# Half steps spread among the whole ones, and one shared step moved from the expert phase to the begin of attention

## The chip, the cores and the metric

The kernel runs on one core of a Trainium2 chip. The metric is the time of one execution on the device, in microseconds, the median of several runs.

## What is computed

A transformer block on 16 batches of 512 rows of 256 numbers, float32:

```python
xn = layernorm(x)
# attention: Q, K, V = relu(xn @ W + b), 16 heads, causal, masked softmax
att = gamma * normalise(softmax(Q K^T / 4) V + xn) + beta
# experts: 8 routed ones, each row goes to its best 2, and one shared by all rows
shared = (silu(xn @ sw1) * (xn @ sw3)) @ sw2
moe = sum over the row's 2 experts of cw * (silu(xn @ w1[e]) * (xn @ w3[e])) @ w2[e]
out = x + att + moe + shared
```

Every matrix of the experts is 256x512 or 512x256. To keep float32's precision each operand of a product is cut into a high and a low part of a narrower format, and a product is made as three matmuls: high by high, high by low, low by high.

## The kernel before

There are two phases, each a block of five programs, one for each engine, that meet in counting semaphores. The order of work within an engine is written out by hand.

**Attention (`attention_phase`).** The body runs for i = -3 to 16. In iteration i it attends batch i, computes the row maxima of batch i+1, projects batch i+2 and normalises batch i+3, each where such a batch exists. An iteration has 44 slots s, and tables (`AT_K`, `AT_V`, ...) say at which slot an engine does which piece. So at i = -3 and i = -2 there is only setup, norm and projection, and at i = -1 the row maxima of batch 0 come in. SP's queue issues all loads and stores in order; `load_aug` loads the augmented queries and keys of a batch with 14 DMAs for each half. Rows of the norm are scattered by GpSimd to `expert_rows`, sorted by expert.

**Experts (`ffn_phase`).** Its work is a series of steps. Step 0 is the shared expert on batch 0. Steps 1 to 39 are the routed chunks: 32 whole ones (512 rows of one expert) and then 7 half ones (256 rows). Steps 40 to 54 are the shared expert on batches 1 to 15. Each step n has four tiles m of 128 hidden columns. TensorE does, in this order: up product of tile 0 (`up(n, 0)`), transposes of the next step's rows, the down products of the step before (`down(n-1)`), up products of tiles 1 to 3. For each tile ScalarE computes silu (`sil`), VectorE multiplies (`hf`), ScalarE copies the high part (`hid_h`) and VectorE subtracts to get the low part (`hid_l`). `down` waits for the last `hid_l` of its step; the up product of a tile waits for `h_done` of the tile two before, whose bank it takes.

Around that, in each routed step:

- ScalarE (`cut_high`) and GpSimd (`cut_low`) cut the next step's weights into high and low, in six pieces of 128x512. TensorE's next step begins when four are cut.
- SP loads the rows of step n+2, stores the result of step n-1 (after ScalarE's `copy_result`), and loads the weights of step n+2.
- Attention's second layer norm is spread over pairs of steps, one batch for each pair. SP's `load_norm` brings its rows in an odd step and `load_residual` the residual; GpSimd's `norm_sum`, `norm_root` and `norm_beta`, VectorE's `norm_centre` and ScalarE's `norm_squares` run in the even step behind; ScalarE's `norm_scale`, GpSimd's `norm_end` and SP's `store_norm` in the step after that. The loads of a norm take the tiles of the one before:

```python
def load_norm(pair):
    sp.wait_ge(norm_read, pair)
...
def norm_end(pair):
    pool.wait_ge(y_scaled, pair)
    pool.wait_ge(res_ready, pair)
    pool.wait_ge(norm_stored, 16 * pair)
    gp.tensor_tensor(out_whole, out_y, out_res, ALU.add).then_inc(norm_read, 1)
```

In the shared steps GpSimd gathers each row's two expert results by indirect DMA, and VectorE adds them, weighted, to the output tile (`complete`), and adds the shared result (`add_shared`).

Of the kernel before, what the change touches and what calls it, by code (L numbers as in the profile page):

```python
# [92 lines left out]
def attention_phase(nc, t, part_dram, xn_dram, expert_rows, plan):  # L93
# [28 lines left out]
    with ExitStack() as ctx:  # L122
# [6 lines left out]
        def sem(name):  # L129
# [34 lines left out]
        q_aug = [sb(f"q_aug{i}", [P, H, S], BF16) for i in range(2)]  # L164
# [6 lines left out]
        negT = sb("negT", [P, 2, 2, Q], BF16)  # L171
        pT = [sb(f"pT{j}", [P, GH, S - P * j]) for j in range(NT)]
        oTs = sb("oTs", [P, 2, S])
        rsum = sb("rsum", [P, NT, GH])

        brow, browp, rw_sb = oTs[0:1, 0], oTs[0:1, 1], pT[0][0:E, 0, 0:C]
        y = sb("y", [P, NT, C])

        logits = sb("logits", [P, B, NT, E])
        xrow = sb("xrow", [P, 2, NT, C])  # L180
# [12 lines left out]

        s_ps = [ps(f"s_ps{i}", [P, S]) for i in range(3)]
        st_ps = [ps(f"st_ps{i}", [P, S]) for i in range(2)]
        misc = [ps(f"misc{i}", [P, 512]) for i in range(2)]
        oT = ps("oT", [P, 512])

# [13 lines left out]
             "filled gate_differs gate_grown").split()]  # L212

# [67 lines left out]

        def group_at(i):
            return (i - 2) // GB if i >= 2 and (i - 2) % GB == 0 and i < B else None
# [30 lines left out]
        def _(sp):  # L314
# [55 lines left out]
            def load_early_rows():  # L370

                sp.dma_start(plan["raw"][:, 3 * 4 * C:].rearrange("p (t c) -> p t c", c=C),
                             xn_dram[0].rearrange("(t p) c -> p t c", p=P)).then_inc(plan["x_in"], 16)
# [31 lines left out]
            def body(i, par, tail, attend, maxima, project, norm):  # L405
                if maxima:
# [234 lines left out]
        def _(act):  # L641
# [36 lines left out]
            def key_ones(k):  # L678

                await_(act, ones_ready, 1)  # L680
                rows_ = k_aug[k][ROW_MASK:P].rearrange("p h (a n) -> p (h a) n", n=P)
                fn(rows_, ones[ROW_MASK:P].rearrange("p (o n) -> p o n", o=1).to_broadcast([P - ROW_MASK, H * S // P, P]),
                   ACT.Copy).then_inc(pads, 1)

            key_ones(0)
# [9 lines left out]
            def body(i, par, tail, attend, maxima, project, norm):  # L695
                for s in range(NU):
# [19 lines left out]
                    if s == AT_SQUARE and norm:  # L716
                        await_(act, a_ready, i + 4)
                        fn(ln_t[:], ln_a[:], ACT.Square).then_inc(sq_done, 1)
                        if i == -3:
                            key_ones(1)  # L720
# [11 lines left out]
        def _(dve):  # L732
# [58 lines left out]
            def weights(s):  # L791
# [7 lines left out]
                if s == AT_ROUTER:  # L799
                    split_router()  # L800

# [343 lines left out]
            def body(i, par, tail, attend, maxima, project, norm):  # L1145
                for s in range(NU):
# [6 lines left out]
                    if tail:  # L1153
                        if s == AT_NORMALISE[3]:
                            normalise(i - 1, 3)
                    if project:
# [73 lines left out]
                    if i == -3:  # L1230
                        weights(s)

# [3 lines left out]
        def _(pe):  # L1236
# [35 lines left out]

            def row_scores(b, par, u):

                if u % NU2 == 0:
# [32 lines left out]
            def weigh(b, par, g, pair):  # L1308

                if (g, pair) == (0, 0):  # L1310
                    await_(pe, vaug_done, b + 1)
                await_(pe, exp_done, NU * b + last_unit[g, 2 * pair + 1] + 1)
# [26 lines left out]
            def body(i, par, tail, attend, maxima, project, norm):  # L1339
                for s in range(NU):  # L1340
# [8 lines left out]
                    if project:  # L1349
# [20 lines left out]
                        if s == AT_K[3]:  # L1370
                            await_(pe, qf_ready, 2 * NC * b + 1)
                            project_tile(b, 3)
                    if s == AT_ROWS[0] and attend:
# [53 lines left out]
def ffn_phase(nc, t, part_dram, xn_dram, expert_rows, plan, out):  # L1427
# [17 lines left out]
    STEPS = CHUNKS + B  # L1445
    assert CHUNKS % 2 == 1 and WHOLE == 2 * B and HALVES >= 2
    ACC, GOT = 4, 3
    first_sum = nc.dram_tensor("first_sum", (S, C), F32, kind="Internal").ap()
    expert_results = nc.dram_tensor("expert_results", (WHOLE * S + HALVES * S // 2, C), F32, kind="Internal").ap()

    with ExitStack() as ctx:
# [51 lines left out]

        def width(n):

            return S // 2 if known(n) and WHOLE < n <= CHUNKS else S
# [5 lines left out]
        def routed(engine, step, written_out=False):  # L1512
# [6 lines left out]
            for n in range(1, 5):  # L1519
                step(n, n % 2, (n + 1) // 2, 1 if n >= 3 else None)  # L1520
            if written_out:
                for n in range(5, 2 * B + 1):
                    step(n, n % 2, (n + 1) // 2, (n - 1) // 2)
            else:
                with engine.Fori(2, B) as pair:
                    for odd in range(2):
                        step(pair * 2 + odd + 1, 1 - odd, pair + 1, pair)
# [582 lines left out]
```

## Time and profile before

| | |
|---|---|
| time, median of 3 runs | 1851.2 us (1849.96 to 1851.47) |
| the profiled execution's own time | 1853.11 us |
| its span | 1851.3 us |
| TensorE busy | 1708.6 us, 92% |
| VectorE, ScalarE, GpSimd busy | 1267.1, 1091.7, 1178.7 us |
| TensorE's granted clock over the span | 0.976 of full |

The span is the time from the first to the last instruction that the profile saw. PE is TensorE, PEld its weight load, DVE VectorE, ACT ScalarE, POOL GpSimd, SP the queue that issues DMAs. A busy share is an average over two phases with different limits, so single stretches matter more. Times in a timeline are microseconds from the span's begin. `early_*` and `w_*` are the two buffers of weights, of the even and the odd steps.

### The profile page before, as it was taken

The page shows a single profiled execution, that of the slowest core. Times are in us where ns is not written, and L with a number is a line of the kernel's source. Part 1 is how long each engine was busy: PE and PEld are TensorE (multiplying, and loading weights), DVE is VectorE, ACT ScalarE, POOL GpSimd, SP SyncE. Part 2 cuts the span into 40 slices and gives each one's busy share as a digit, 9 for nine tenths or more (in the row PEclk, how much of TensorE's full clock was granted, in tenths as well). Part 3 has the DMA queues.
Part 4 walks back from the last instruction along what each step waited for, and adds up shares of the span by engine and source line. Part 5 has one row for each costly group of instructions (what it writes and reads, how often), then busy time and mean ns, then how long its engine had stood idle before and what let it go on. Part 6 is the DMA issues. An engine that isn't in the chain of part 4 may idle for free.

```text
span 1851.3 us, 35725 instructions
## 1 busy us (share of the span) xinstructions
PE 1708.6 (92%) x12066; PEld 1287.0 (70%) x12066; DVE 1267.1 (68%) x3089; ACT 1091.7 (59%) x2072; POOL 1178.7 (64%) x1441
## 2 busy tenths in 40 slices
PE   3489999998999899999799999999999999999998
PEld 2255555555555555554488888888888888888887
DVE  6888888888888888877544554455455454566666
ACT  5247567666676566766556666666666666333332
POOL 4466557776677667846257777777777787553443
PEclk9689999999999999999899999999999999999999
DMA  1444445444445454454655766756667675465543
GB/s 54 154 127 122 129 128 173 154 156 157 144 150 162 141 171 150 159 171 172 221 189 180 237 191 201 232 192 212 216 197 222 200 229 188 149 188 149 158 146 99
DMA packets 246374, 313.29 MB, mean 169 GB/s; under 512 B 31546, under 2 KB 210884, under 8 KB 240068
## 3 DMA queue, kind: packets, MB, share of 16 engines
q1 hardware_dynamic: 233924, 277.60, 47.3%
q0 software_dynamic: 12288, 33.57, 5.7%
q8 instruction: 96, 1.57, 0.3%
q14 instruction: 66, 0.54, 0.1%
HBM read 211.70 MB, written 98.86 MB: 168 GB/s over the span
## 4 chain that ended last, share of the span: by engine, by line
PE 47%; ACT 1%; DMA 1%; DVE 1%; POOL 1%; issue 0%; SPq 0%; DVEq 0%; ACTq 0%
PE gu L2006 29%; PE yp L2020 15%; PE xt L1995 2%; DMA early_raw<-in_L_ffn_w_dram 0%; DVE hf L1876 0%; DMA early_raw<-in_L_ffn_sw_dram 0%; ACT early_high L1771 0%; ACT sil L1777 0%; ACT hid_h L1779 0%; POOL early_low L1679 0%; POOL early_down L1679 0%; POOL w_up_l L1679 0%; POOL rows L1740 0%; DVE hid_l L1879 0%; ACT xc L1785 0%
## 5 line engine op out<-in xcount | busy, mean ns | idle before, releaser
L650 ACT ACTIVATE pT<-st_ps 128x512 f32<-128x512 f32 x682 | 368.6, 563 | 265.7 <-PE st_ps L1305 258.9
L923 DVE CUSTOM_DVE_ANT_0 s_ps<-s_ps,masks 128x384 f32<-128x384 f32 (+1 forms) x512 | 314.6, 633 | 39.6 <-PE s_ps L1284 34.1
L2006 PE MATMUL gu<-xc,early_high 128*128 128x512 f32 (+1 forms) x1120 | 337.9, 385 | 2.5 <-DVE xc L1887 1.5
L1876 DVE TENSOR_TENSOR hf<-sil,gu 128x512 f32<-128x512 f32 (+1 forms) x220 | 143.7, 653 | 275.9 <-ACT sil L1777 275.9
L1284 PE MATMUL s_ps<-k_aug,q_aug 97*128 97x512 bf16 (+3 forms) x1024 | 262.2, 309 | 37.9 <-DVE mx L923 23.4
L1303 PE MATMUL st_ps<-q_aug,k_aug 99*128 99x512 bf16 (+1 forms) x992 | 268.9, 303 | 11.8 <-ACT pT L650 6.7
L1879 DVE TENSOR_TENSOR hid_l<-hf,hid_h 128x512 fp32r<-128x512 f32 (+1 forms) x220 | 175.1, 796 | 147.7 <-ACT hid_h L1779 147.7
L2006 PEld LDWEIGHTS gu<-xc,early_high 128*128 128x128 f32 x1120 | 205.4, 190 | 44.4 <-POOL early_low L1679 4.0
L1779 ACT ACTIVATE hid_h<-hf 128x512 fp32r<-128x512 f32 (+1 forms) x220 | 133.1, 605 | 174.2 <-DVE hf L1876 174.2
L1777 ACT ACTIVATE sil<-gu 128x512 f32<-128x512 f32 (+1 forms) x220 | 123.9, 563 | 180.5 <-PE gu L2006 180.5
L2006 PE MATMUL gu<-xc,early_low 128*128 128x512 f32 (+1 forms) x560 | 214.3, 383 | 0.0
L1687 POOL DMA_INDIRECT got<-expert_results,place x128 | 124.1, 969 | 140.6 <-DVE hf L1876 115.4
L2020 PE MATMUL yp<-early_down,hid_h 128*128 128x256 f32 x1072 | 198.6, 287 | 4.7 <-DVE hid_l L1879 3.0
L1305 PE MATMUL st_ps<-masks,identb 128*128 128x128 bf16 x992 | 194.2, 221 | 0.0
L2006 PE MATMUL gu<-xc,w_up_h 128*128 128x512 f32 (+1 forms) x640 | 184.1, 373 | 6.7 <-DVE hf L1876 3.9
L1318 PE MATMUL oT<-pT,v_aug 128*32 128x512 f32 (+3 forms) x2048 | 170.9, 452 | 2.1 <-ACT pT L650 1.3
L2020 PEld LDWEIGHTS yp<-early_down,hid_h 128*128 128x128 f32 x1072 | 167.9, 193 | 6.2 <-DVE hid_l L1879 3.9
L1284 PEld LDWEIGHTS s_ps<-k_aug,q_aug 97*128 97x128 bf16 x1024 | 95.7, 99 | 107.9 <-DVE mx L923 43.9
L482 POOL DMA_INDIRECT expert_rows<-xrow,slot x128 | 126.7, 990 | 63.6 <-issue 30.3
L1679 POOL TENSOR_TENSOR early_low<-early_raw,early_high 128x512 fp32r<-128x512 f32 x80 | 102.3, 1300 | 87.9 <-ACT early_high L1771 87.9
L2020 PE MATMUL yp<-early_down,hid_l 128*128 128x256 f32 x536 | 152.4, 284 | 0.0
L926 DVE TENSOR_REDUCE mx<-s_ps 128x2 f32<-128x512 f32 (+1 forms) x192 | 123.6, 681 | 19.5 <-PE s_ps L1284 18.9
(260 smaller groups left out, 3889.5 us busy)
## 6 DMA issues: line engine op xcount, KB each, us to landing
w_raw<-in_L_ffn_w_dram SPq DMA_DIRECT2D x60, 512.0 KB, 6.5
early_raw<-in_L_ffn_w_dram SPq DMA_DIRECT2D x57, 512.0 KB, 5.7
part_scr<-parts SPq DMA_DIRECT2D x64, 384.0 KB, 3.8
q_aug<-part_scr SPq DMA_DIRECT2D x192, 128.0 KB
k_aug<-part_scr SPq DMA_DIRECT2D x192, 128.0 KB
early_raw<-expert_rows SPq DMA_DIRECT2D x34, 512.0 KB
expert_results<-yo SPq DMA_DIRECT2D x32, 512.0 KB, 3.3
x_sb<-in_L_attn_x_dram SPq DMA_DIRECT2D x16, 512.0 KB, 4.1
```

The source lines that it names most:

```text
L482: gp.indirect_dma_start(expert_rows, bass.IndirectOffsetOnAxis(ap=at, axis=0), xrow[:, b % 2, n], None).then_inc(scattered[b % 2], 16)
L650: fn(pT[j][:, h:h + heads], unit_view(column_bank(b, u), heads, w), ACT.Exp).then_inc(exp_done, 1)
L923: vec.tensor_tensor_reduce(bank[:, 0:keys], bank[:, 0:keys], masks[:, 2 * C + P - keys:2 * C + P], 1.0, LOWEST, ALU.add, ALU.max, mx[:, h ...
L1284: last = mm(v[:, n], q_aug[par][0:ROWS_S, h0 + n, P * q:P * (q + 1)], k_aug[par][0:ROWS_S, h0 + n, 0:keys], start=heads == 1, stop=n == he ...
L1303: mm(v[:, n], k_aug[par][0:ROWS_ST, h, P * j:P * (j + 1)], q_aug[par][0:ROWS_ST, h, P * j:S], start=True, stop=False)
L1305: last = mm(v[:, n, 0:P], identb[:], cmask[:, 1], start=False, stop=True)
L1318: last = mm(oT[32 * n:32 * (n + 1), P * j:S], v_rows[par][:, at:at + 32], pT[j][:, n], start=j == 0, stop=j == NT - 1, tile_position=(0, 3 ...
L1779: fn(hid[par][0][:, m, 0:w], hf[:, m % 2, 0:w], ACT.Copy).then_inc(hh_done, 1)
L1876: vec.tensor_tensor(hf[:, m % 2, 0:w], sil[:, m % 2, 0:w], gu[m % 2][:, 1, 0:w], ALU.mult).then_inc(h_done, 1)
L1879: vec.tensor_tensor(hid[par][1][:, m, 0:w], hf[:, m % 2, 0:w], hid[par][0][:, m, 0:w].bitcast(F32), ALU.subtract).then_inc(hl_done, 1)
L2006: last = mm(gu[m % 2][:, a, 0:width(n)], w_up[wpar][x][:, a, c, P * m:P * (m + 1)], xc[par][:, y, c, 0:width(n)], start=k == 0, stop=k == ...
L2020: last = mm(yp[:, i], hid[par][x][:, m, P * i:P * (i + 1)], w_dn[wpar][y][:, m], start=j == 0, stop=j == 3 * NH - 1)
```

## The change

Two things are done in one kernel.

1. In the expert phase each half step stands behind four whole ones, at steps 5, 10, 15, 20, 25, 30 and 35, in place of 33 to 39. `chunk_of` says which chunk a step takes, and the loop over pairs is written out. Norms begin in even steps that are whole (`NORM_AT`); even half steps (10, 20, 30) have none. In a half step that is odd `norm_end` is put behind all six pieces of `cut_low`.
2. The shared expert on batch 0 is computed in iterations -2 and -1 of attention: weights and x are loaded by SP at the begin into memory that is lent from tiles used later, cut by ScalarE and VectorE, and the four up tiles, silu, products and down products are put at slots of their own. Step 0 of the expert phase takes batch 1 instead, and the last shared steps take batches 2 to 15: there are 54 steps. The completing of batches is redistributed (`COMPLETED`, `LATE`, `TWICE`).

```diff
+        AT_SW_UP, AT_SW_DOWN, AT_SW_ADD = (18, 19, 30, 35), (10, 14), (12, 16)
+        AT_SW_LOW = (34, 11)
+        AT_SW_SILU, AT_SW_HH = (21, 21, 30, 36), (22, 23, 32, 38)
+        AT_SW_H, AT_SW_HL = (20, 21, 27, 31), (22, 24, 28, 33)
+        AT_ONES = 25
...
+            for a, (n, rows_) in enumerate((("sw1", C), ("sw3", C), ("sw2", 2 * C))):
+                sp.dma_start(sw_raw[:, a].rearrange("p (c n) -> p c n", c=rows_ // P),
+                             t[n][0].rearrange("(c p) n -> p c n", p=P)).then_inc(sw_in, 16)
+            sp.dma_start(sw_sum[:], t["x"][0].rearrange("(t p) c -> p t c", p=P)).then_inc(sw_x_in, 16)
...
+                if b == 1 and tt == 0:
+                    await_(sp, sw_added, 2)
...
+            def shared_high():
+                await_(act, sw_in, 48)
+                await_(act, rw_ps, 1)
+                for q in range(SW_PIECES):
+                    high, _, raw = sw_piece(q)
+                    fn(high, raw, ACT.Copy).then_inc(sw_high, 1)
+            def shared_silu(m):
+                await_(act, sw_gu_ready, m + 1)
+                fn(sw_sil[:, m % 2], sw_gu[m % 2][0][:], ACT.Silu).then_inc(sw_silu, 1)
...
+            def shared_h(m):
+                await_(dve, sw_silu, m + 1)
+                vec.tensor_tensor(sw_hf[:, m % 2], sw_sil[:, m % 2], sw_gu[m % 2][1][:], ALU.mult).then_inc(sw_h, 1)
+            def shared_hid_low(m):
+                await_(dve, sw_hh, m + 1)
+                vec.tensor_tensor(sw_hid[1][:, m], sw_hf[:, m % 2], sw_hid[0][:, m].bitcast(F32), ALU.subtract
+                                  ).then_inc(sw_hl, 1)
+            def shared_add(h):
+                await_(dve, sw_y_ready, h + 1)
+                at = sw_sum[:, 2 * h:2 * h + 2]
+                vec.tensor_tensor(at, sw_y, at, ALU.add).then_inc(sw_added, 1)
...
             def row_scores(b, par, u):
+                if b == 0 and u == 2:
+                    await_(pe, sw_h, NH)
...
-    STEPS = CHUNKS + B
+    STEPS = CHUNKS + B - 1
+    COMPLETED, LATE = {3: (0, 1), 4: (2,), 5: (3,)}, 5
+    TWICE = 20
...
+        SPACING = WHOLE // HALVES + 1
+        NO_NORM = tuple(n for n in range(SPACING, CHUNKS + 1, SPACING) if n % 2 == 0)
+        NORM_AT = {n: k + 1 for k, n in enumerate(n for n in range(2, CHUNKS, 2) if n not in NO_NORM)}
+        def half_step(n):
+            return 0 < n <= CHUNKS and n % SPACING == 0
+        def chunk_of(n):
+            return WHOLE + n // SPACING if half_step(n) else n - n // SPACING
...
+            for n in range(1, CHUNKS + 1):
+                step(n, n % 2, NORM_AT.get(n + n % 2), NORM_AT.get(n - 2 + n % 2))
...
                 cut_low(n + 1, 1 - par, (0, 1))
-                if par == 1 and ends is not None:
+                if par == 1 and ends is not None and not half_step(n):
                     norm_end(ends)
                 if par == 0 and begins is not None:
                     norm_root(begins)
                 cut_low(n + 1, 1 - par, range(2, PIECES))
+                if par == 1 and ends is not None and half_step(n):
+                    norm_end(ends)
                 if par == 0 and begins is not None:
                     norm_beta(begins)
...
-                if 2 <= c < 4:
+                for b in COMPLETED.get(c, ()):
                     for k in range(2):
-                        complete(c - 2, k)
+                        complete(b, k)
```

## Rows read from the trace of the kernel before

**Rows 1.** Engines' summary and costliest groups of the page (busy us, mean ns | idle before).
```profile
PE 1708.6 (92%) x12066; PEld 1287.0 (70%) x12066; DVE 1267.1 (68%) x3089; ACT 1091.7 (59%) x2072; POOL 1178.7 (64%) x1441
...
L1876 DVE TENSOR_TENSOR hf<-sil,gu 128x512 f32<-128x512 f32 (+1 forms) x220 | 143.7, 653 | 275.9 <-ACT sil L1777 275.9
```

**Rows 2.** The chain that ended last, expert phase (start us, us, what).
```profile
1455.12 10.97 PE gu L2006 x48
...
1466.96 5.76 PE yp L2020 x48
1472.72 10.99 PE gu L2006 x48
...
1581.41 2.87 PE yp L2020 x24
1584.29 10.91 PE gu L2006 x48
...
1601.83 10.92 PE gu L2006 x48
```

**Rows 3.** Busy times by stretch: step 32 to the end of step 40.
```profile
1480.74:1592.45 111.71, 103.82 (x742) 96.36 (x742) 55.85 (x96) 70.99 (x162) 75.70 (x62) 0.98 0.60 195
```

**Rows 4.** Groups of instructions: the weighted adds of gathered results.
```profile
L1942 DVE SCALAR_TENSOR_TENSOR acc<-got,gate,acc 128x256 f32<-128x256 f32 x128 | 53.4, 479 | 2.1 <-DMA got<-expert_results,place 1.5
```

**Rows 5.** Timeline of PE, first half step, 33 (start us, us, what [idle before]).
```profile
1498.25 0.44 PE L2006 MATMUL gu<-xc,w_up_h 128*128 128x256 f32 x2
...
1501.71 0.48 PE L2020 MATMUL yp<-early_down,hid_h 128*128 128x256 f32 x2 [1.40 <-POOL w_dn_l L1679]
```

**Rows 6.** Timeline of ACT, half step 33.
```profile
1510.45 1.01 ACT L1851 ACTIVATE yo<-yp 128x1024 f32<-128x1024 f32 x1
1511.36 0.37 ACT L1777 ACTIVATE sil<-gu 128x256 f32<-128x256 f32 x1
```

**Rows 7.** Timeline of DVE, half step 33.
```profile
1504.09 1.32 DVE L1879 TENSOR_TENSOR hid_l<-hf,hid_h 128x256 fp32r<-128x256 f32 x1 [0.48 <-ACT hid_h L1779]
...
1511.83 0.42 DVE L1876 TENSOR_TENSOR hf<-sil,gu 128x256 f32<-128x256 f32 x1 [0.57 <-ACT sil L1777]
```

**Rows 8.** Timeline of POOL, half step 33.
```profile
1503.82 2.74 POOL L1679 TENSOR_TENSOR early_low<-early_raw,early_high 128x512 fp32r<-128x512 f32 x2
1507.31 2.41 POOL L1740 TENSOR_TENSOR rows<-rows 128x1024 f32<-128x1024 f32 x1 [0.75 <-ACT rows L1858]
```

**Rows 9.** Timeline of POOL, an odd whole step and the even one behind it.
```profile
1225.62 2.40 POOL L1740 TENSOR_TENSOR rows<-rows 128x1024 f32<-128x1024 f32 x1
...
1236.98 2.85 POOL L1706 TENSOR_TENSOR rows<-rows 128x1024 f32<-128x1024 f32 x1
...
1249.14 2.55 POOL L1679 TENSOR_TENSOR w_up_l<-w_raw,w_up_h 128x512 fp32r<-128x512 f32 x2 [1.04 <-ACT w_up_h L1771]
```

**Rows 10.** Timeline of SP in the odd step of rows 9: issue of the norm's second load.
```profile
1228.66 0.87 SPq L1582 DMA_DIRECT2D rows<-layernorm_rows  x1
```

**Rows 11.** DMA issues from 1226 to 1246 us (KB each, us to landing).
```profile
rows<-attention_sum SPq DMA_DIRECT2D x1, 512.0 KB, 4.4
rows<-layernorm_rows SPq DMA_DIRECT2D x1, 512.0 KB, 5.8
```

**Rows 12.** Timeline of DVE, the even step of rows 9.
```profile
1241.50 1.20 DVE L1901 TENSOR_REDUCE sm<-rows 128x4 f32<-128x1024 f32 x1
```

**Rows 13.** Timeline of ACT, the even step of rows 9.
```profile
1244.96 1.00 ACT L1851 ACTIVATE yo<-yp 128x1024 f32<-128x1024 f32 x1
1246.56 0.60 ACT L1777 ACTIVATE sil<-gu 128x512 f32<-128x512 f32 x1 [0.59 <-PE gu L2006]
```

**Rows 14.** The chain that ended last, step 1 of the expert phase.
```profile
932.72 4.50 PE gu L2006 x12
```

**Rows 15.** Timeline of DVE, iteration -2 of attention.
```profile
51.43 0.18 DVE L834 RECIPROCAL sm<-sm 128x4 f32<-128x4 f32 x1 [2.07 <-POOL sm L526]
...
62.06 1.67 DVE L880 SCALAR_TENSOR_TENSOR xn<-ln_t,sm,ln_q 128x256 f32<-128x256 f32 x4
```

More of the change, by code:

```diff
@@ L163, in attention_phase @@
         vtmp = sb("vtmp", [P, NT, C])
-        q_aug = [sb(f"q_aug{i}", [P, H, S], BF16) for i in range(2)]
+        q_aug0 = sb("q_aug0", [P, H, S], BF16)
         k_aug = [sb(f"k_aug{i}", [P, H, S], BF16) for i in range(2)]
@@ L719, in body @@
                         if i == -3:
-                            key_ones(1)
+                            shared_high()
+                            key_ones(1, 0, H * 3 // 4)
+                    if i == -2:
+                        for m in range(NH):
+                            if s == AT_SW_SILU[m]:
+                                shared_silu(m)
+                        for m in range(NH):
+                            if s == AT_SW_HH[m]:
+                                shared_hid(m)
+                        if s == AT_ONES:
+                            key_ones(1, H * 3 // 4, H // 4).then_inc(pads, 1)
                     if s == AT_COPY[2] and attend:
@@ L1155, in body @@
                             normalise(i - 1, 3)
+                    if i == -2 and s == AT_SW_LOW[1]:
+                        shared_low(range(3, SW_PIECES))
+                    if i == -1 and s in AT_SW_ADD:
+                        shared_add(AT_SW_ADD.index(s))
                     if project:
@@ L1231, in body @@
                         weights(s)
+                        if s == AT_SW_LOW[0]:
+                            shared_low(range(0, 3))
+                    if i == -2:
+                        for m in range(NH):
+                            if s == AT_SW_HL[m]:
+                                shared_hid_low(m)
+                            if s == AT_SW_H[m]:
+                                shared_h(m)
             iterations(dve, body)
@@ L1639, in shared_step @@
             def shared_step(n, par, c):
-                if c == 1:
+                if c == 2:
                     store_result(CHUNKS)
-                    for k in range(3):
+                    store_norm(B)
+                    for k in range(ACC):
                         load_acc(k)
@@ L1659, in _ @@
             load_routed(2, 0)
-            routed(sp, routed_step)
+            routed(routed_step)
             shared(shared_step)
@@ L1691, in gathers @@
             def gathers():
-                for j in range(2 * NT):
-                    pool.wait_ge(h_done, NH * (CHUNKS + 1) + NH - 1 + j // 2)
-                    gather(j // NT, j % NT)
-                for c in range(2, B):
-                    for i in range(NT):
-                        pool.wait_ge(h_done, NH * (CHUNKS + c) + 1 + i)
-                        gather(c, i)
+                for p in range(B * NT):
+                    after = p // 2 if p < TWICE else p - TWICE // 2
+                    pool.wait_ge(h_done, NH * (CHUNKS + 1) + NH - 1 + after)
+                    gather(p // NT, p % NT)
             def norm_sum(pair):
@@ L1756, in _ @@
             pool.wait_ge(params_in, 32)
-            routed(pool, step)
+            routed(step)
             pool.wait_ge(y_stored, 16 * (CHUNKS + 1))
@@ L1862, in _ @@
             first_step()
-            routed(act, routed_step)
+            routed(routed_step)
             shared(shared_step)
@@ L2054, in _ @@
             routed_step(0, 0, None, None)
-            routed(pe, routed_step, written_out=True)
+            routed(routed_step)
             shared(shared_step)
```

162 lines of the change are left out of this document (111 added, 51 removed).

## The prediction, as it was made before the result

> **What bounds the kernel now.** I read the summary of the engines first, then the chain that ended last, then the stretch of the half steps engine by engine. TensorE is busy for 92% of the span [rows 1]. In the expert phase it is more than busy: the chain runs through TensorE alone, one whole step every 17.60 us (10.97 in the up products, 5.76 in the down products of the step before, the rest transposes), and one shared step every 17.54 us [rows 2]. So a step taken out of this phase is worth its full price, and a stall put into it costs its full price. The stretch from the start of step 32 (the last whole one) to the start of step 41 (the second shared one) lasts 111.71 us with TensorE busy for 103.82 [rows 3]; it holds one whole step, seven half steps and one shared step. All that spreading the half steps can win lies there. In the attention phase VectorE and TensorE share the bound, so I count a delay of its begin at its full size.
>
> **The change, part by part.**
>
> *One shared step fewer.* STEPS falls from 55 to 54; the last shared step and all around it stay as they are, so this takes 17.54 us out [rows 2]. The additions of gathered results (`complete`) are moved: two batches one behind the other after step 41. A batch costs VectorE eight instructions of 0.479 us, 3.8 us [rows 4]; two are 7.7 us, against 17.54 us of the step with some 7 us of other VectorE work between them and the next tile that TensorE waits for. I take 0; without that cover it would be 3.8 us once.
>
> *A half step among whole ones.* The trace has one such place, step 33 behind step 32. TensorE starts its first up product at 1498.25 and then stands idle for 1.40 us before the down products of the whole step 32 [rows 5] (the row names a piece of GpSimd, but `hl_done` is waited for at the same place): the up product of a half tile is too short to cover silu, product, high and low of the last tile. At the other end, ScalarE copies the whole result at 1510.45 before silu of tile 2 at 1511.36 [rows 6], and VectorE's product of that tile ends at 1511.83 + 0.42 = 1512.25 [rows 7]; the next step's first up product needs it. From 1498.25 to 1512.3 are 14.05 us. Each of the seven half steps now stands behind a whole one, so each has this length. The order of GpSimd's work in it is changed (norm_end last), but VectorE's product binds at 14.05 anyway.
>
> *The whole step behind it* has the down products of a half step: 17.60 - 5.76 + 2.87 = 14.7 us [rows 2]. Behind the half steps 10, 20 and 30 no layer norm begins or ends, and I take 14.7.
>
> *The whole step behind half steps 5, 15, 25 and 35* is another matter. NORM_AT puts the begin of a norm into steps 6, 16, 26 and 36, and its rows are loaded in the half step before. Two things stand ahead of that load. (1) load_norm waits for norm_read, which the norm_end of the norm before raises; that one now runs in the same half step, behind all six cut_low. In time from the half step's start: GpSimd starts the first two pieces at 1503.82, +5.6, and two pieces take 2.74 [rows 8]; six are done at +13.8; norm_end takes 2.41 [rows 8] and ends at +16.2, when the half step has been over for 2 us. (2) The second load is issued 0.63 us behind the end of norm_end (1225.62 + 2.40 against 1228.66) [rows 9, 10] and the two landed 4.4 and 5.8 us after their issue [rows 11]. That is +21.2 to +22.7, I take +21.9, or 7.9 us into the whole step. GpSimd's norm_sum, 2.85 us [rows 9], is first in its queue, ahead of the cuts of the next weights, and ends at 10.7. From there the chain of the step is as in the trace: VectorE's reduction starts at 1241.50 [rows 12], ScalarE's copy_result at 1244.96, behind the squares (3.46 later) [rows 13]; a half result costs some 0.5 us to copy; silu of tile 1 starts at 1246.56 [rows 13] and GpSimd's fourth piece ends at 1249.14 + 2.55, 5.13 us later [rows 9]. Together 9.1 us, so the weights of the next step are cut at 7.9 + 2.85 + 9.15 = 19.9 us. TensorE would be through with the step at 14.7. It waits for `h_done` of tile 1, then for these weights. Queued behind the waiting norm_sum are all cut_low of the step; behind VectorE's wait for the sum its tiles 1 to 3; behind ScalarE's wait for the row sums copy_result and tile 1, for which TensorE waits.
>
> During such a wait TensorE idles for about 4 us. In step 1, behind a wait of a few us, twelve up products took 4.50 us [rows 14] where a quarter of a whole step's up products is 2.74: the clock had fallen to its lower level. A small part of that lies on this chain, since the cuts come later than the products; I add 0.4 us. So this step has 20.3 us. The Trainium skill (TensorE: Matmul & The Clock Gate, What's actually happening) says that the default clock is the throttled one and activity releases it; here the trace agrees with 4.50 against 2.74. By that rule alone each of the four waits would cost the full 1.8 us, 5 or 6 us more in the sum.
>
> Bounds of this step: from below 16.4 us, if the rows are there in time (in the trace VectorE comes to the reduction at 1241.50, which is 7.2 us into its step, fourteen steps of 17.60 ahead of 1480.74; 9.15 follow); from above 22.4 (5.8 us to land and the full 1.8 of the clock). I take 20.3, from the middle of the landings.
>
> *Sum of the routed part.* Before, step 32 to 40 and six whole steps that will follow half ones: 111.71 + 6 x 17.60 = 217.3. After, the same fifteen steps: 7 x 14.05 + 3 x 14.7 + 4 x 20.3 + 17.54 = 241.2. That is +23.9 us. Even at 14.7 for all seven followers it would be +1.6: the 5 us of idle around step 40 are won back, and seven short covers are paid.
>
> *The first batch's shared step in attention.* TensorE (96 products), ScalarE and GpSimd have room there; VectorE is what counts. It gets six low cuts, four products, four hid_l and two adds, 16 instructions of 128x512, at 0.653 [rows 1] 10.4 us. Much is hidden in waits: VectorE idles 2.07 us before 51.43 [rows 15] alone. Not hidden are, as I read the slots: tile 3's product and hid_l, which stand behind the last norm work at 62.06 [rows 15] and ahead of the first row maximum, with ScalarE's piece between, 2 us; the two adds, 1.3 us; and some 0.7 because values_out(2) now waits for TensorE's tile 2, with the reciprocals behind it. I take +4. Bounds: 1.3 (only the adds) and 10.4 (all). The four loads (2 MB) are issued behind those that the begin waits for, and the wait of load_aug for sw_added ends before SP gets there; I take 0.
>
> The Trainium skill (SBUF, State Buffer; Who interferes with whom) says that a VectorE instruction with two SBUF inputs contends with a GpSimd one that reads SBUF. In the trace hid_l took 1.32 us beside GpSimd's cuts where the product, one input from PSUM, took 0.42 at the same shape [rows 7]. By that rule the four hid_l added in attention could cost up to 3.6 us more, 1865 in all.
>
> **Total.** 23.9 - 17.5 + 4 = +10.4. The profiled execution spans 1851.3 us, as the median of the runs, 1851.2 (its own time is 1853.1, with 1.8 us around the span). So about 1861.7 us.
>
> **Rivals.**
> A. The norm is not late: loads land before GpSimd is ready, and steps 6, 16, 26, 36 have 16.4 us. The sum is then 23.9 - 15.6 - 17.5 + 4 = -5.2, 1846 us. For it: in the trace norm_sum never waits for its rows. Against it: there norm_end runs in the middle of a 17.6 us step. It decides from 16.8 us of that step on down (faster by 0.2%); break-even is at 17.7.
> B. The price is half as large, 16.8 to 18.6 us for that step: 1847.5 to 1855. Landings as short as 4.4 are not enough for it; GpSimd would have to be through 2 us earlier.
> C. The begin of attention bears all of VectorE's new work: 10.4 in place of 4, 1868 us; with the upper bound of the four steps 1876. For it: VectorE is hardly idle there. Against: the waits on GpSimd's small operations are there to be filled.
> D. Spreading wins as meant, with followers at 14.7 and nothing late: 1.6 - 17.5 + 4, 1839 us. The chain that I found speaks against it.
>
> **How the numbers follow.** My case, 1856 to 1867 us, has 0.60; A 0.13, B 0.12, C 0.10, D 0.05. A measurement of this kernel can tell 0.2%, 3.7 us, from no change. Slower: 0.60 + 0.10 + a little of B, 0.72. Within: 0.11. Faster: A and D, 0.17. The range for 8 in 10 leaves out D and half of A below, and the far end of C above: 1846 to 1870. The likeliest case alone has 1856 to 1867.
>
> **What would show it.** Steps 5, 10, ... would start to end in about 14 us with some 1.4 us idle before the down products. Steps 6, 16, 26, 36 would show norm_sum at 7 to 9 us into the step, a wait of GpSimd on the loads ahead of it, and TensorE idle for 4 to 5 us; steps 11, 21, 31 none of it. Steps 39 to 41 would run without the stall of before. The first row maximum would come 2 or 3 us later, and the expert phase would begin 4 us later. The prediction is wrong if norm_sum starts on time, or if the half steps are shorter than 13.6 us, or if attention's begin moves by 8.

## The result

The changed kernel took 1876.2 us (median of 4 runs, 1874.81 to 1878.44), the kernel before 1850.9 beside it (4 runs, 1849.96 to 1851.47). The ratio is 1.0139, with a 95% interval of 1.0125 to 1.0153: slower, as predicted, but by 25 us in place of 10, and outside the range of 1846 to 1870.

The profiled execution of the changed kernel had its own time of 1874.81 us and a span of 1873.1, 21.8 more than the span of before. The sums below are of spans; the 3.5 us between 21.8 and 25.3 are, but for 0.1, how the two profiled executions lie to their medians (the one of before 2.2 above, this one 1.4 below). Two single executions, 9337 us in experiment 1 and 5810 us in experiment 2, lie far outside all others and count in no ratio below.

The page's summary and its group of VectorE's products, which answer to [rows 1]: nothing in the busy times tells of 22 us. TensorE is busy 8.8 us longer, VectorE 0.9 us shorter.

```profile
PE 1717.4 (92%) x12058; PEld 1290.7 (69%) x12058; DVE 1266.2 (68%) x3094; ACT 1095.8 (59%) x2079; POOL 1180.2 (63%) x1441
...
L2028 DVE TENSOR_TENSOR hf<-sil,gu 128x512 f32<-128x512 f32 (+1 forms) x216 | 140.9, 652 | 282.1 <-ACT sil L1929 282.1
```

The transposes of the next step's rows come once in each step, so the distance between them times the steps. Here are those of the changed kernel in steps 14 to 17, of which 15 is a half one: 16.29, 15.56 and 19.38 us.

```profile
1169.14 0.60 PE L2147 MATMUL xt<-ident,early_raw 128*128 128x128 f32 x4
1185.43 1.04 PE L2147 MATMUL xt<-ident,early_raw 128*128 128x128 f32 x8
1200.99 1.04 PE L2147 MATMUL xt<-ident,early_raw 128*128 128x128 f32 x8
1220.37 1.03 PE L2147 MATMUL xt<-ident,early_raw 128*128 128x128 f32 x8
```

Busy times by stretch (columns: stretch, length, then busy us of PE, PEld, DVE, ACT, POOL, granted clock, DMA share, GB/s): those three intervals, and the same three around the even half step 20.

```profile
1169.14:1220.37 51.23, 46.79 (x285) 41.12 (x284) 27.84 (x41) 32.63 (x73) 39.14 (x40) 0.97 0.66 211
1255.74:1302.40 46.66, 45.14 (x285) 40.21 (x284) 18.84 (x31) 28.23 (x55) 28.07 (x21) 1.00 0.63 209
```

By my terms the first is 17.6 + 14.05 + 20.3 = 51.95, the second 17.6 + 14.05 + 14.7 = 46.35. The chain that ended last, in step 16 of the changed kernel, is the one of the prediction up to silu of tile 1; it answers to [rows 8] and to [rows 9, 10, 12, 13].

```profile
1197.37 2.55 POOL rows L1890
1199.92 0.02 issue
1199.94 0.37 SPq L1727
1200.31 0.04 issue
1200.35 5.01 DMA rows<-layernorm_rows
1205.37 0.07 issue
1205.43 2.40 POOL rows L1856
...
1207.93 1.23 DVE sm L2053
...
1213.30 7.24 PE gu L2158 x24
```

norm_end (L1890) ends at 1199.92, the second load is issued at once and lands 5 us later, norm_sum (L1856) starts at 1205.43, and TensorE goes on at 1213.30, after 2.92 us idle. The prediction let the step end with a second wait, for the cuts of the next weights. The fourth of these ends at 1217.45, TensorE takes up the next step at 1217.51 without an idle time, so the two ends fall together. From there back to the step's first up product at 1198.17 are 19.3 us. So this part came nearly as written. What I had not foreseen stands at both ends of the expert phase. First its begin: the first transposes of before and of the changed kernel.

```profile
912.40 1.94 PE L1995 MATMUL xt<-ident,early_raw 128*128 128x128 f32 x8 [4.38 <-PEq L122]
```

```profile
923.23 1.94 PE L2147 MATMUL xt<-ident,early_raw 128*128 128x128 f32 x8 [4.51 <-PEq L122]
```

It comes 10.8 us later, where I had 4. Then the change from the routed steps to the shared ones: the chain that ended last, from step 40 on.

```profile
1617.81 1.03 ACT yo L2003
1618.85 0.02 issue
1618.87 0.36 SPq L1751
1619.22 0.04 issue
1619.27 4.35 DMA attention_sum<-rows
1623.62 0.07 SPq L1720
1623.68 0.04 issue
1623.72 9.40 DMA early_raw<-layernorm_rows
1633.12 0.04 issue
1633.17 1.97 PE xt L2147 x8
```

SP stores the result of step 39, stores the last norm (which in the kernel before was done many steps earlier), issues four loads of acc (L1720, 512 KB each) and only then the load of step 42's rows. It needs 9.4 us to land. TensorE's transposes come 22.18 us behind those before them, the next ones 18.88 and 17.80 us, in place of 17.54: 6.2 us.

The account by spans:

| part | on record | measured |
|---|---|---|
| begin of the expert phase | +4 | +10.8 |
| steps 0 to 2 | 0 | -0.6 |
| seven half steps, their followers, step 40 | +23.9 | +22.4 |
| other whole steps | 0 | +0.8 |
| rows of step 42 late | 0 | +6.2 |
| one shared step fewer | -17.5 | -17.5 |
| tail | 0 | -0.4 |
| sum | +10.4 | +21.7 |

The third line: the seven groups of three intervals last 4 x 31.84 + 78.03 in all with an odd half step and 3 x 46.66 with an even one, 345.4 us; less seven whole steps of 17.6 and with a shared step of 17.54 that is 239.7, where I had 241.2, against 217.3 of before.

### The profile page after: what moved, and what is told of

It reads as the page before. It is cut to its first block, busy times and chain, and to the rows that moved or that the text cites. A ratio compares the mean times of both kernels' runs of the same rounds, so it can differ in the third digit from the quotient of the medians.

```text
span 1873.1 us, 34800 instructions
## 1 busy us (share of the span) xinstructions
PE 1717.4 (92%) x12058; PEld 1290.7 (69%) x12058; DVE 1266.2 (68%) x3094; ACT 1095.8 (59%) x2079; POOL 1180.2 (63%) x1441
## 4 chain that ended last, share of the span: by engine, by line
PE 38%; POOL 5%; ACT 3%; DMA 2%; issue 2%; DVE 1%; SPq 0%; DVEq 0%; POOLq 0%
PE gu L2158 23%; PE yp L2172 13%; PE xt L2147 2%; POOL early_low L1832 1%; DMA rows<-layernorm_rows 1%; POOL early_down L1832 1%; DVE hf L2028 1%; POOL got L1840 1%; ACT sil L1929 1%; POOL rows L1861 1%; ACT hid_h L1931 1%; POOL rows L1890 1%; POOL w_dn_l L1832 1%; POOL rows L1856 1%; DMA early_raw<-layernorm_rows 1%
## 5 line engine op out<-in xcount | busy, mean ns | idle before, releaser
L2158 PE MATMUL gu<-xc,early_high 128*128 128x512 f32 (+1 forms) x1088 | 332.9, 389 | 14.7 <-DVE hf L2028 13.2
L2031 DVE TENSOR_TENSOR hid_l<-hf,hid_h 128x512 fp32r<-128x512 f32 (+1 forms) x216 | 168.8, 782 | 144.8 <-ACT hid_h L1931 144.8
L2158 PEld LDWEIGHTS gu<-xc,early_high 128*128 128x128 f32 x1088 | 200.9, 192 | 58.6 <-DVE hf L2028 13.8
L2158 PE MATMUL gu<-xc,early_low 128*128 128x512 f32 (+1 forms) x544 | 209.9, 386 | 0.0
L2172 PE MATMUL yp<-early_down,hid_h 128*128 128x256 f32 x1040 | 191.7, 286 | 7.5 <-POOL w_dn_l L1832 4.1
L2172 PEld LDWEIGHTS yp<-early_down,hid_h 128*128 128x128 f32 x1040 | 162.2, 192 | 9.8 <-POOL w_dn_l L1832 4.9
L2172 PE MATMUL yp<-early_down,hid_l 128*128 128x256 f32 x520 | 147.2, 283 | 0.0
```

The costliest lines, as they stand in the source:

```text
L2031: vec.tensor_tensor(hid[par][1][:, m, 0:w], hf[:, m % 2, 0:w], hid[par][0][:, m, 0:w].bitcast(F32), ALU.subtract).then_inc(hl_done, 1)
L2158: last = mm(gu[m % 2][:, a, 0:width(n)], w_up[wpar][x][:, a, c, P * m:P * (m + 1)], xc[par][:, y, c, 0:width(n)], start=k == 0, stop=k == ...
L2172: last = mm(yp[:, i], hid[par][x][:, m, P * i:P * (i + 1)], w_dn[wpar][y][:, m], start=j == 0, stop=j == 3 * NH - 1)
```

## The experiments

Each kernel ran with five rounds beside the kernel before. Ratios are to that, with the 95% interval; the changed kernel has 1.0139.

**1. Attention's part alone.** The half steps go back behind the whole ones, and with them the norms' steps, the place of `norm_end` and the last norm's store (the diff shows the line that decides).

```diff
-            return 0 < n <= CHUNKS and n % SPACING == 0
+            return WHOLE < n <= CHUNKS
```

> The shared step of batch 0 stays in attention (54 steps), the half steps go back to 33 to 39. Read from the two traces, the begin of attention costs 12.2 us where it happens (2.4 in the first loads, 4.2 in iteration -2, 5.5 in iteration -1) and the expert phase begins 10.8 us later; one shared step less is -17.5. My account: 1851 + 10.8 - 17.5 = 1844, ratio 0.996, and within 1842 to 1847. If the term on record (4 us) were right and the rest came from the combination with the spread: 1837. If the steps written out one by one cost 0.05 to 0.08 us each (17.68 in place of 17.60 in the trace), the whole steps show 17.68 here too; if spreading costs it, 17.60.

1850.2 us, ratio 0.9995 (0.9986 to 1.0004). The expert phase began at 920.39. My 1844 was missed: one shared step less, -17.5, is eaten up by +8 at the begin, +2 in whole steps of 17.68 us (not from the spread, then), some +2 around step 40 (0.59 of it TensorE's wait for the rows of step 42, ahead of which four loads of acc stand here too) and +3 in the first half step. That last one is a collision. VectorE's hid_l in the first fence below takes 2.61 us, its likes 0.69, and GpSimd's norm_beta in the second runs from 1511.31 to 1513.66:

```profile
1511.60 2.61 DVE L2026 TENSOR_TENSOR hid_l<-hf,hid_h 128x512 fp32r<-128x512 f32 x1 [0.70 <-ACT hid_h L1926]
```

```profile
1511.31 2.35 POOL L1858 TENSOR_TENSOR rows<-rows,beta_b 128x1024 f32<-128x1024 f32 x1
```

hid_l ends 0.55 us behind norm_beta, as if it had not begun before. The Trainium skill (SBUF, State Buffer; Who interferes with whom) calls the port pair that the two share an exclusive lock, and this trace agrees with 2.61 against 0.69. TensorE stood idle there for 3.72 us, in place of 1.40 in the kernel before.

**2. The spread alone**, put into the kernel before: attention as before and 55 steps.

```diff
-            return S // 2 if known(n) and WHOLE < n <= CHUNKS else S
+            return S // 2 if half_step(n) else S
```

> The half steps are spread, the shared step of batch 0 stays in the expert phase (55 steps), attention is that of before. My account from the traces: spreading 22, whole steps 0.05 us longer each 1, late rows of the second shared step up to 6 (here three loads stand behind the store of the last norm, not four): 1851 + 22 + 1 + 4 to 6 = 1878 to 1880, ratio 1.015. By the terms on record, spread alone: 1875. If the stall of the second shared step needs the fourth load: 1874.

1878.3 us, ratio 1.0149 (1.0130 to 1.0167), as expected. So the two parts are nearly separate: 27.5 and -0.6 us, together 26.9 against 25.3 measured. The rows of step 42 were late here as well (an interval of 19.76 us), with three loads of acc.

**3. Rows of step 42 first.**

```diff
                 if c == 2:
+                    load_x(n + 2, xn_dram[c + 2])
                     store_result(CHUNKS)
                     store_norm(B)
...
-                if c < B - 2:
+                if 2 < c < B - 2:
```

> As the changed kernel, but in step 40 the rows of step 42 are loaded ahead of the store of the last norm and of the four loads of acc. My account: the step that shows 22.2 us falls to 17.6 and the one behind it from 18.9 to 17.6, -6 us against the changed kernel: 1870, ratio 1.0105. Rival: the rows are late because the DMA engines are full of gathers and stores then, whatever the order: 1876, ratio 1.014.

1873.1 us, ratio 1.0109 (1.0092 to 1.0127), 5.6 us less by the ratios, 3.1 by the medians. The trace shows the stall gone: 17.68 and 17.54 us.

```profile
1597.60 1.04 PE L2148 MATMUL xt<-ident,early_raw 128*128 128x128 f32 x8
1615.28 1.03 PE L2148 MATMUL xt<-ident,early_raw 128*128 128x128 f32 x8
1632.82 1.04 PE L2148 MATMUL xt<-ident,early_raw 128*128 128x128 f32 x8
```

The order in SP's queue was the cause. The span fell by 1.8 us only, though, because the followers of the half steps 25 and 35 took 20.68 and 20.62 us here and the steps behind them 18.53 and 18.64, 4.0 us more in all than in the changed kernel. TensorE's wait in step 26 was as long as there (2.88 and 2.97 us); what differs is the clock granted behind it, as the same stretch of the changed kernel and of this one shows:

```profile
1354.00:1391.00 37.00, 32.63 (x201) 28.52 (x201) 20.15 (x28) 22.31 (x50) 29.58 (x26) 0.95 0.65 210
```

```profile
1354.00:1391.00 37.00, 32.72 (x193) 28.70 (x193) 19.77 (x27) 22.10 (x50) 29.70 (x26) 0.91 0.65 213
```

**4. norm_end early** in the odd half steps, behind the first two pieces of cut_low.

```diff
-                if par == 1 and ends is not None and not half_step(n):
+                if par == 1 and ends is not None:
                     norm_end(ends)
```

> As the changed kernel, but in the odd half steps norm_end stands behind the first two pieces of cut_low, as in the whole steps. It then ends 5.4 us earlier, and the four other pieces 2.4 us later. My account: steps 6, 16, 26 and 36 lose most of their stall of 4.7 us, and the late pieces give back a part: 10 to 16 us less than the changed kernel, 1860 to 1866, ratio 1.005 to 1.008. Rival: what the late pieces cost the next step is as much as what is won: 1876. Rival: the stall of these steps is not from the norm: 1876 too, but norm_sum would start 5 us earlier in the trace and the steps stay at 19.5.

1871.8 us, ratio 1.0116 (1.0100 to 1.0131): 4.4 us less, not 10 to 16. The followers took 18.2 to 18.7 us. The chain tells what was late next: the norm's loads (L1727) stood behind the store of the last result (L1751), and this waited for copy_result (L2001), which in a half step comes between tiles 1 and 2.

```profile
1189.83 1.02 ACT yo L2001
1190.86 0.37 SPq L1751
1191.23 0.05 issue
1191.29 0.50 SPq L1727
1191.79 0.04 issue
1191.83 6.28 DMA rows<-layernorm_rows
1198.10 0.07 issue
1198.17 2.41 POOL rows L1856
```

**5. Steps written out**, in the kernel before.

```diff
-                with engine.Fori(2, B) as pair:
-                    for odd in range(2):
-                        step(pair * 2 + odd + 1, 1 - odd, pair + 1, pair)
+            for n in range(5, 2 * B + 1):
+                step(n, n % 2, (n + 1) // 2, (n - 1) // 2)
```

> The kernel before, with its loop over pairs of steps written out on every engine (before, only TensorE's is); nothing else is changed. In the kernel with the shared step in attention and the half steps at the end, 28 whole steps show 17.68 us in place of 17.60 to 17.64, and the first half step is 3 us longer, because VectorE's hid_l falls upon GpSimd's norm_beta (2.61 us in place of 0.77). If writing out is the reason for the first: +2 us, and +5 if the 3 us come with it: 1853 to 1856, ratio 1.001 to 1.003. If not: 1851, steps of 17.60 to 17.64.

1851.6 us, ratio 1.0004 (0.9995 to 1.0012). The steps do take 17.68 us in place of 17.60 to 17.64, as these two intervals show, but the total can't be told from that of before. The 3 us did not come: the first half step was as long as before.

```profile
1093.69 1.03 PE L1990 MATMUL xt<-ident,early_raw 128*128 128x128 f32 x8
1111.38 1.04 PE L1990 MATMUL xt<-ident,early_raw 128*128 128x128 f32 x8
1129.06 1.03 PE L1990 MATMUL xt<-ident,early_raw 128*128 128x128 f32 x8
```

**6. Down products in four pieces** in attention.

```diff
-        AT_SW_DOWN, AT_SW_ADD = (10, 14), (12, 16)
+        AT_SW_DOWN, AT_SW_ADD = (12, 14, 20, 22), (16, 25)
...
```

> As the changed kernel, but the down products of the first batch's shared step in iteration -1 come in four pieces of 12 at slots 12, 14, 20 and 22 in place of two of 24 at 10 and 14, and the two adds at 16 and 25. My account: VectorE was idle for 4.05 and 3.58 us behind the two pieces, for which the row scores behind them in TensorE's queue were late; pieces half as long are mostly covered by the three score banks. 3 to 4.5 us less than the changed kernel: 1872 to 1873, ratio 1.0115 to 1.012. Rival: VectorE's own added work sets the begin of attention, and nothing is won: 1876.

1875.7 us, ratio 1.0135 (1.0120 to 1.0149): nothing. Between the first row maximum and the negated maxima 3.6 us were won, but the first maximum came 2.0 us later in this trace, and 2.4 us were lost again behind the negated maxima. 0.9 of these are a wait that I had made: SP's loads for batch 1, issued at 105.65, wait until the lent memory is free (in the changed kernel they followed the issue before them at once), and I had moved the second add there.

```profile
104.89 0.69 DVE L897 TENSOR_TENSOR sw_sum<-oT,sw_sum 128x512 f32<-128x512 f32 x1
```

```profile
105.65 0.54 SPq L429 DMA_DIRECT2D q_aug<-part_scr  x1
```

**7. Shared loads held** until the biases have landed.

```diff
+            await_(sp, rows_in, 80)
             for a, (n, rows_) in enumerate((("sw1", C), ("sw3", C), ("sw2", 2 * C))):
```

> As the changed kernel, but SP issues the four loads for the shared step (2 MB) only when the biases have landed. My account: these loads share the DMA engines with the first ones, and the first transposes start at 10.57 us in place of 8.12; now they start at 8.1 and all of attention is 2.4 us earlier: 1873.8, ratio 1.0125. The weights arrive some 4 us later, so ScalarE's first cuts start near 19 us, and its work until 30 still fits. Rival: they come too late and what is won is lost: 1876.

1877.3 us, ratio 1.0137 (1.0122 to 1.0152): missed. TensorE's first product came at 7.87 us, 2 us earlier, but only 1.1 us of it was left at the row maxima (70.21 against a mean of 71.29), and nothing at the expert phase. The table of marks below shows why the first number misleads: with a clock about as low in between as here, experiments 3 and 8 had the first maximum at 72.5, 2.3 us later. Later in this trace two followers of half steps took 20.6 us, as in experiment 3, 4.0 us more with the steps behind them.

**8. norm_end early and the norm's loads ahead of the store.**

```diff
+                first = half_step(n) and par == 1 and begins is not None
+                if first:
+                    load_norm(begins)
                 store_result(n - 1)
...
```

> As the changed kernel, with norm_end early in the odd half steps and, besides, the norm's two loads ahead of the store of the last result in SP's queue there. With norm_end early alone, the trace shows the loads still behind that store, which waits for copy_result between tiles 1 and 2 of the half step: issued at +12.7 us of it, landed 6.3 us later, and steps 6, 16, 26, 36 still take 18.4 us in place of 19.4. My account: now the rows are there before the step begins, and these steps fall to the lower bound on record, 16.4: 3 us less each than the changed kernel, 12 in all, 1864, ratio 1.007. Rival: squares and copy_result hold the step at 18.4 even then: 1872.

1865.2 us, ratio 1.0067 (1.0053 to 1.0082), as expected. The follower's interval is 16.53 us:

```profile
1198.51 1.04 PE L2148 MATMUL xt<-ident,early_raw 128*128 128x128 f32 x8
1215.04 1.03 PE L2148 MATMUL xt<-ident,early_raw 128*128 128x128 f32 x8
```

So late norm rows cost the changed kernel 11 us by the medians (13 by the ratios), behind two waits and not one.

**9 to 12. Kernels put together of these pieces.** 9, 10 and 12 have the half steps last (edit 1), the loop over pairs as in the kernel before, and edit 3; 9 and 12 have the down products in four pieces, 9 has edit 7. 11 is the changed kernel with edits 3, 7, 8 and the pieces. The slots of the pieces are now:

```diff
-        AT_SW_DOWN, AT_SW_ADD = (10, 14), (12, 16)
+        AT_SW_DOWN, AT_SW_ADD = (12, 14, 19, 21), (16, 23)
```

> The kernel before in the order of its routed steps (whole ones in a loop, then the seven half ones), with the first batch's shared step in attention, 54 steps, and three mends: the shared loads held until the biases have landed, the down products in four pieces (slots 12, 14, 19, 21, adds at 16 and 23), and the rows of step 42 loaded ahead of the four loads of acc. Worked out from the marks of eight traces: the changed attention brings the expert phase 10.3 us later, the held loads give back 1.1, the four pieces 0 to 1; one shared step less is -17.5; the second shared step no longer waits for its rows, -2 to 0: 1841 to 1844, ratio 0.995. If the shared step in attention costs as much as it saves: 1851.

1838.8 us, ratio 0.9938 (0.9922 to 0.9953): 12 us faster than the kernel before, the fastest of all, and 2 us below what I expected.

> The same without the two mends in attention: half steps last, steps in the loop, shared step of batch 0 in attention as in the changed kernel, rows of step 42 loaded first. Against the run with written-out steps (1850.2) I count -2 for the loop, -2 for the rows, and 0 to -3 for the first half step, where VectorE had waited for GpSimd's norm_beta: 1843 to 1846, ratio 0.997. It tells how much of the next run's gain is from the two mends in attention (1 to 2 us, about what can be told).

1843.9 us, ratio 0.9969 (0.9957 to 0.9981), as expected.

> The changed kernel with all mends together: norm_end early and the norm's loads first in odd half steps (-11 alone), rows of step 42 first (-3 to -6 alone), shared loads held and down products in four pieces (-1 to -2). If the terms are separate: 1876 - 11 - 5 - 1.5 = 1858, ratio 1.004. What remains above the kernel with the half steps last is the price of spreading as such: seven half steps with their followers at 31.4 and 29.0 us against 27.3 (9.73 + 17.6) in a row, less what the row loses at its two ends, some 10 to 14 us.

1853.3 us, ratio 1.0017 (1.0009 to 1.0026). All mends together give 23 us, 5 more than the sum of what I had for each, and the spread kernel is still not ahead of the kernel before. From the third transposes of the expert phase to those of step 41 it takes 669.84 us, experiment 10 takes 657.85: spreading as such costs 12 us, some 1.5 of it from steps written out. By the medians, 11 and 9, which has the same mends in attention, lie 14.5 us apart.

> The run that came out fastest (0.9938) without its held loads: half steps last, rows of step 42 first, down products of the shared step in four pieces with the adds at slots 16 and 23. The same without the pieces had 0.9969. In the changed kernel the pieces alone, with the second add at slot 25, won 3.6 us up to the negated maxima and lost them again: SP's loads for batch 1 wait for that add (issued at 105.65, the add ended at 105.5). If that was the reason, the pieces with the add at 23 now give 3 to 4 us: ratio 0.995. If the gain of the fastest run comes from the held loads: 0.997 here.

1843.4 us, ratio 0.9951 (0.9938 to 0.9965). It lies between 9 and 10 and can't be told from either, so how the 0.3% between these two are shared between the pieces and the held loads stays open. Its expert phase began at 925.3 us, the latest of all traces, in an execution of 1847.6 us, the slowest of its five.

**The marks in attention**, from the traces of all these (mean start in us; before: 3 traces, the kernel before and experiments 2 and 5; changed: 5, experiments 1, 3, 4, 8 and the changed kernel):

| mark | before | changed | later by | exp. 6 | exp. 7 | exp. 9 | exp. 10 | exp. 11 | exp. 12 |
|---|---|---|---|---|---|---|---|---|---|
| first product of TensorE | 8.10 | 9.89 | 1.8 | 10.25 | 7.87 | 8.38 | 10.60 | 8.25 | 9.81 |
| first row maximum | 64.74 | 71.29 | 6.5 | 73.26 | 70.21 | 70.90 | 73.69 | 68.89 | 72.92 |
| first negated maxima | 92.02 | 104.06 | 12.0 | 102.40 | 102.98 | 99.68 | 103.46 | 97.67 | 102.72 |
| first column scores | 111.07 | 122.46 | 11.4 | 123.24 | 121.40 | 118.17 | 121.90 | 116.19 | 121.35 |
| expert phase | 911.1 | 921.4 | 10.3 | 922.5 | 923.8 | 917.9 | 921.2 | 917.5 | 925.3 |

From TensorE's first product to the first maximum there are 56.4 to 57.0 us before. With the new work there are two values: 60.6 to 60.7 in four traces (the changed kernel, 1, 4, 11) and 62.3 to 63.1 in the seven others. The granted clock between 52 and 58 us is 1.00 in the four and 0.72 to 0.81 in the seven. VectorE waits there for a product that stands behind an up tile in TensorE's queue, 1.68 us in the changed kernel and 3.25 in experiment 10:

```profile
57.53 0.42 DVE L1012 TENSOR_TENSOR vtmp<-misc,bv_b 128x256 f32<-128x256 f32 x1 [1.68 <-PE misc L1359]
```

```profile
59.99 0.42 DVE L1012 TENSOR_TENSOR vtmp<-misc,bv_b 128x256 f32<-128x256 f32 x1 [3.25 <-PE misc L1359]
```

From the first maximum to the negated ones there are 27.3 us before, 32.8 in the changed kernel in each of the five traces, and 29.8 in experiment 10, whose attention is the same code. What differs is the clock while the down products run: the two pieces of 24 take 4.0 and 4.4 us in the one, 2.9 and 2.95 in the other. Since the first maximum came 2.4 us later in experiment 10, its negated maxima are only 0.6 us ahead of the mean: the time of low clock lay elsewhere, and its cost with it. Busy times by stretch, changed kernel and experiment 10:

```profile
78.00:84.00 6.00, 5.54 (x28) 5.17 (x29) 2.76 (x5) 1.26 (x2) 2.12 (x6) 0.72 0.27 90
...
90.00:96.00 6.00, 6.00 (x32) 5.39 (x32) 1.49 (x5) 0.67 (x2) 2.32 (x7) 0.74 0.01 3
```

```profile
78.00:84.00 6.00, 4.33 (x26) 3.40 (x25) 5.21 (x12) 1.86 (x3) 0.58 (x3) 0.92 0.34 113
...
90.00:96.00 6.00, 5.96 (x40) 5.24 (x41) 2.96 (x9) 1.46 (x3) 3.04 (x8) 1.00 0.02 3
```

VectorE's waits in the changed kernel are for the row scores queued behind these products on TensorE; in experiment 10 they are 2.56 and 2.10 us. All its waits for row scores in this stretch add up to 8.9 us in the changed kernel, 5.9 in experiment 10 and 0.9 in the kernel before.

```profile
84.81 0.57 DVE L1020 CUSTOM_DVE_ANT_0 s_ps<-s_ps,masks 128x384 f32<-128x384 f32 x1 [4.05 <-PE s_ps L1418]
...
94.02 0.57 DVE L1020 CUSTOM_DVE_ANT_0 s_ps<-s_ps,masks 128x384 f32<-128x384 f32 x1 [3.58 <-PE s_ps L1418]
```

With the pieces of 12 the stretch takes 28.8 us in experiments 9 and 11, where the clock was low in parts of it too (0.68 between 80 and 84 us and 0.60 between 92 and 96 in experiment 9), and 29.1 and 29.8 in 6 and 12, where it was full from 80 to 96. So the pieces give 4 us where the clock is low, and 0 to 0.6 against experiment 10 where it is full; of the 3.6 us of experiment 6 up to 3.0 can be the clock.

## Why the prediction was wrong, step by step

- **One shared step fewer, -17.5:** right. The steps behind it are 17.54 us as before, and moving `complete` cost nothing.
- **A half step behind a whole one, 14.05:** right. Step 15 takes 14.27 us from its first up product to the next step's, and the three intervals around a half step are within 0.8 us of my sum. The idle time before the down products was 1.02 us, not 1.4.
- **Followers of even half steps, 14.7:** right, 14.81.
- **Followers of odd half steps, 20.3:** nearly right, 19.4 to 19.7. The mechanism was the one predicted, and norm_sum started 7.3 us into the step. The 0.4 us for the clock was too small and did no harm: behind its wait TensorE took 7.24 us for 24 up products, where half of 48 is 5.5, so 1.8 us in all, but by then it had lost 2.92 us and not 4, and the cuts of the weights bound as long. In the traces of experiments 3 and 7 the lower clock lasted longer in two of the four steps, and these took 20.6 us. One thing in it I had named but not weighed: the store of the last result ahead of the loads. Experiment 4 shows that it would have held the rows up alone, experiment 8 that both together are the stall.
- **"TensorE (96 products), ScalarE and GpSimd have room there; VectorE is what counts": this step failed.** I took +4; it was +10.3 (mean of five traces). Up to the first maximum it is 4.7 us beside the late first loads. Of these, tile 3's product and hid_l ahead of the first maximum are the 2.0 us that I had (69.25 to 71.24 in the changed kernel); but where I had 0.7 for the wait for TensorE's tile 2, VectorE waits 1.68 to 3.25 us. How the rest is shared was not tried. Between the maxima, 5.5 us, VectorE was idle more than before, because TensorE's 24 down products in one piece stood ahead of the row scores, for 4.0 and 4.4 us, part of it at the lower clock (the same pieces at the full clock, in experiment 10, cost 2.5 of the 5.5). TensorE has room there on average, but not in pieces of 4 us with VectorE three score banks behind it. My upper bound of 10.4 held the number, and rival C gave its size, but for another reason.
- **"The four loads ... I take 0": wrong by 1.8 us.** They are issued behind those that the begin waits for, and still TensorE's first product, which waits for the last bias, came at 9.89 us in place of 8.10; with the four held back, in experiment 7, it came at 7.87. The wait of load_aug for sw_added did cost nothing; in experiment 6, with the add later, it cost 0.9 us.
- **The change to the shared steps: a term that was missing.** I had written that steps 39 to 41 would run without the stall of before. The last norm ends one step before the shared ones now, its store and four loads stand in SP's queue ahead of step 42's rows: 6.2 us. Experiment 3 took them away.
- **Rival A** (norm not late, 16.4 us) did not come, but experiment 8 makes it come, with 16.5 us: my lower bound of that step was right.

In the account, +6.8 at the begin and +6.2 at the seam, with -1.5, -0.6, +0.8 and -0.4 for the rest, are the 11.3 us between 10.4 and 21.7. That the begin moved by 8 or more stands among the things that I had said would make the prediction wrong.

## What to carry to other kernels

Work moved into a phase where an engine is half idle can still hold up the engine that sets the pace, if it comes in pieces longer than the buffers between the two; here shorter pieces took most of that wait away, though what they give in the total stays open. Price such work at both levels of the clock. When a step is taken out or put elsewhere, read again every queue at the seam: what is issued ahead of the next step's first load counts, a store that was long done before too. And when one wait is taken away, name the next one in the same queue before pricing the gain: experiment 4 gave a third of what I expected for that reason, and experiment 6 ran into such a wait too.

## What the runs showed of the hardware

- A VectorE instruction on SBUF took 2.61 us in place of 0.69 beside one of GpSimd of 2.35 us, and TensorE stood for 3.72 us; which instructions meet changes with a shift of a few hundred ns, and the same steps showed nothing of it in experiments 5 and 10. In experiment 1 hid_l came 0.29 us behind the start of norm_beta; in experiment 5 it came 0.07 us ahead of it, took 0.69, and norm_beta took 2.89.
- With the loop written out on ScalarE, VectorE, GpSimd and SP, a whole step of unchanged work took 17.68 us in place of 17.60 to 17.64. Why was not tried.
- The same 24 products of 256 columns took 4.4 us in the changed kernel and 2.95 in experiment 10, with nothing else changed but the granted clock (0.74 and 1.00 in the stretch). Between executions of one attention code the expert phase began at 917.3 to 923.2 us, so a term of 2 us there needs the mean of several traces.
- One and the same wait of TensorE, 2.9 us in the follower of half step 25, was followed by a step of 19.69 us in the changed kernel and of 20.68 in experiment 3, at a granted clock of 0.95 and 0.91 in the stretch around it.
